# Deformable sampling on one core: tents in one VectorE operation, distances on GpSimd, and first weights, transposes and products placed earlier

## The reference

```python
xr = relu(x)                                     # x: normed input, B=8, C=32, H=W=16
om = conv3x3(xr, w_off) + b_off                  # 54 channels: 3 x (DG=2 groups) x (9 taps)
o1, o2, m = split(om, 3, axis=1)
ys = o1 + base_y;  xs = o2 + base_x              # where each tap of each position samples
mask = sigmoid(m)
sampled = bilinear(xr, ys, xs)                   # 0 outside the image
sampled = sampled * mask
out = einsum('bgcphw,ogcp->bohw', sampled, w) + b
out = (out - mean(out)) * rsqrt(var(out) + 1e-5) * gamma + beta
```

## Time and profile before

| | us |
|---|---|
| median of three runs | 128.83 |
| span of the profiled execution | 127.3 |
| first offsets written | 57.65 |
| first part of step 0's weights begins | 63.82 |
| transposes of step 3 begin | 74.31 |
| transposes of step 11 begin | 99.40 |
| batch statistics begin | 105.23 |

### The profile page before, as it was taken

How to read it: one execution, slowest core, us unless ns; L and a number is a source line. 1 busy time by engine, 2 the same in 40 slices (tenths; PEclk the granted TensorE clock), 3 DMA queues, 4 the chain that set the end, 5 groups by cost and what they waited for, 6 DMA issues and landing times.

```text
span 127.3 us, 3032 instructions
## 1 busy us (share of the span) xinstructions
PE 114.2 (90%) x1200; PEld 82.3 (65%) x1201; DVE 74.4 (58%) x149; ACT 68.3 (54%) x121; POOL 25.9 (20%) x34
## 2 busy tenths in 40 slices
PE   6989889998989899997977899999999987989990
PEld 5667566577423325877966678888888975656750
DVE  0076976718984362129999599699493004346241
ACT  4254796357630407027978959969956631347000
POOL 8996000004940000002616050050000000000000
PEclk9999999999999999999999999999999999999997
DMA  3544000000101000000000000000000000000002
GB/s 106 168 56 110 12 0 5 0 1 8 34 0 31 3 17 14 5 5 0 0 0 5 0 0 5 0 0 5 0 8 0 0 8 0 0 0 0 5 0 88
DMA packets 3060, 2.22 MB, mean 17 GB/s; under 512 B 1570, under 2 KB 2754, under 8 KB 3040
## 3 DMA queue, kind: packets, MB, share of 16 engines
q0 software_dynamic: 464, 0.67, 2.7%
q1 hardware_dynamic: 2144, 0.74, 2.4%
q10 hardware_dynamic: 432, 0.55, 1.2%
HBM read 1.68 MB, written 0.26 MB: 15 GB/s over the span
## 4 chain that ended last, share of the span: by engine, by line
PE 59%; DVE 21%; ACT 12%; issue 6%; DVEq 0%; ACTq 0%
PE ps L977 9%; PE ps L489 5%; DVE smat L913 5%; PE ps L991 5%; PE ps L1001 4%; PE ps L1293 4%; PE ps L514 3%; PE ps L496 3%; PE ps L276 3%; PE ps L287 3%; ACT tx L848 2%; DVE smatT L740 2%; PE ps L518 2%; PE ps L655 2%; ACT rstd L530 2%
## 5 line engine op out<-in xcount | busy, mean ns | idle before, releaser
L913 DVE TENSOR_TENSOR smat<-ty,tx 128x1536 f32<-128x1536 f32 (+1 forms) x14 | 21.5, 1555 | 4.3 <-ACT tx L848 4.2
L954 ACT ACTIVATE smatT<-ps 128x1536 f32<-128x1536 f32 x12 | 17.4, 1450 | 7.8 <-PE ps L977 7.6
L977 PE MATMUL ps<-cst,smat 128*128 128x128 f32 x144 | 18.1, 275 | 2.6 <-DVE smat L913 2.3
L977 PEld LDWEIGHTS ps<-cst,smat 128*128 128x128 f32 x144 | 15.7, 140 | 4.3 <-DVE smat L913 3.2
L489 PE MATMUL ps<-cst 128*128 128x256 f32 x48 | 13.0, 387 | 0.3 <-issue 0.3
L1001 PE MATMUL ps<-samp,wc 128*128 128x128 f32 x72 | 11.0, 291 | 0.0
L991 PE MATMUL ps<-smatT,xt 128*32 128x96 f32 x384 | 10.4, 249 | 0.4 <-ACT samp L945 0.4
L1001 PEld LDWEIGHTS ps<-samp,wc 128*128 128x128 f32 x72 | 8.9, 191 | 1.6
L489 PEld LDWEIGHTS ps<-cst 128*128 128x128 f32 x48 | 8.3, 190 | 2.2 <-issue 1.3
L830 POOL TENSOR_SCALAR disty<-disty 128x288 f32<-128x288 f32 x3 | 6.2, 2081 | 17.2 <-ACT disty L837 17.2
L991 PEld LDWEIGHTS ps<-smatT,xt 128*32 128x32 f32 x384 | 7.9, 109 | 2.3 <-issue 1.8
(11 more groups left out here) (200 smaller groups left out, 198.1 us busy)
## 6 DMA issues: line engine op xcount, KB each, us to landing
cst<-in_cst ACTq DMA_DIRECT2D x1, 278.0 KB, 3.5
x<-in_x SPq DMA_DIRECT2D x2, 128.0 KB, 2.9
ew<-in_L_ffn_weight POOLq DMA_DIRECT2D x4, 64.0 KB, 2.2
ew<-in_L_ffn_weight POOLq DMA_DIRECT2D x1, 256.0 KB, 4.2
w<-in_L_ffn_ffn_w SPq DMA_DIRECT2D x3, 64.0 KB
cst<-in_cst ACTq DMA_DIRECT2D x1, 129.0 KB, 3.0
out<-fin SPq DMA_DIRECT2D x1, 128.0 KB, 2.2
out<-fin ACTq DMA_DIRECT2D x1, 128.0 KB, 2.1
```

The costliest lines, as they stand in the source:

```text
L913: return nc.vector.tensor_tensor(smat[:, n % 3, BP * part.start:BP * part.stop, :].rearrange("p u (g r c) -> p (u g) r c", g=DG, c=W), ty[ ...
L954: nc.scalar.activation(smatT[:, n % 2, :, :, :].rearrange("p k g n -> p (k g n)"), ps[:, bank:bank + 3, :].rearrange("p b n -> p (b n)"), ...
L977: last = nc.tensor.transpose(ps[:, bank + u // BP, (u % BP) * P:(u % BP + 1) * P], smat[:, n % 3, u, :], ident)
```

## The change

- **Tents by one VectorE operation.** Distances are now to grid - 1, so d = offset - grid + 1, and `nearness` writes min(2 - d, d) in one `scalar_tensor_tensor`, which is 1 - |offset - grid| without the clipping at 0. Row weights clip (`max` with 0, then times mask). Columns stay unclipped; ScalarE's copy of the turned weights uses Relu instead of Copy, which clips the product. For `jh` = 0 the row tents are ScalarE's, clipped, in two passes.
- **Distances on GpSimd.** `distances_pool` makes all row distances and all column distances, but for those of `jh` = 0 that step 0 needs (`HEAD`, a third, 384 elements), which VectorE makes itself. It waits for `c_oms` of each `jh`. The rest of `jh` = 0 is `TAIL`, 768 elements.
- **Masks.** The sigmoid is Exp, Ln, Exp, three ScalarE operations, one set for `jh` = 0 and one for the other three together.
- **Order.** Six of the window transposes of `jh` = 0 go ahead of the 3x3 convolution, one filler matmul less before them. All window sets are copied by ScalarE. Window sets 1 to 3 go ahead of the fit's transpose. Step 0's transposes and ScalarE's copy of them go ahead of the branch, as do step 1's weights. Step 0's products come before the transposes of step 1. Two `keep_clock` calls of two matmuls go away. PSUM banks are dealt anew (`OMBANK`, `WINBANK`, `FITBANK`, `fit_bank`, `PARTS`).

The diff, cut to its core:

```diff
-OMBANK = (4, 0)
-WINBANK = (5, 1)
+OMBANK = (4, 3)
+WINBANK = (5, 0)
+FITBANK = 3
+PARTS = (1, 2, 0)
+EARLY = 6
...
+        HEAD, TAIL = slice(0, KBG // K), slice(KBG // K, KBG)
+        def column_distances(eng, jh, us, done):
+            shape = [P, us.stop - us.start, W]
+            eng.tensor_tensor(tx[:, jh, us, :], om[:, jh, 1, us].unsqueeze(2).broadcast_to(shape),
+                              const("grid").unsqueeze(1).broadcast_to(shape), ALU.subtract).then_inc(sem(done), 1)
...
+        def distances_pool(pool):
+            pool.wait_ge(sem("c_oms"), 1)
+            row_distances(nc.gpsimd, 0, "p_dy")
+            column_distances(nc.gpsimd, 0, TAIL, "p_dx")
             for jh in range(1, J * NH):
-                pool.wait_ge(sem("p_ay"), jh)
-                d = disty[:, jh, :, :]
-                nc.gpsimd.tensor_scalar(d, d, 1.0, 1.0, ALU.min, ALU.subtract).then_inc(sem("p_ty"), 1)
+                pool.wait_ge(sem("c_oms"), jh + 1)
+                row_distances(nc.gpsimd, jh, "p_dy")
+                column_distances(nc.gpsimd, jh, ALL, "p_dx")
+        def nearness(d, done):
+            nc.vector.scalar_tensor_tensor(out=d, in0=d, scalar=2.0, in1=d, op0=ALU.subtract, op1=ALU.min,
+                                           reverse0=True).then_inc(sem(done), 1)
...
+        def sigmoid_masks(act, link, part):
+            link(nc.scalar.activation(msk[:, part, :], om[:, part, 2, :], ACT.Exp, scale=-1.0))
+            link(nc.scalar.activation(msk[:, part, :], msk[:, part, :], ACT.Ln, bias=1.0))
+            nc.scalar.activation(msk[:, part, :], msk[:, part, :], ACT.Exp, scale=-1.0).then_inc(sem("c_me"), 1)
...
         def fit_dve(dve):
-            for n in range(1, NSTEP):
+            for n in range(2, NSTEP):
                 jh, ki = n // K, n % K
                 if ki == 0:
-                    dve.wait_ge(sem("p_tx"), jh)
+                    dve.wait_ge(sem("s_tx"), jh + 2)
                     dve.wait_ge(sem("s_ty"), jh + 1)
                 if n >= 3:
                     dve.wait_ge(sem("f_tr"), n - 2)
                 step_weights(n).then_inc(sem("f_w"), 1)
-                if ki == 0 and jh + 1 < J * NH:
-                    column_distances(nc.vector, jh + 1, "s_dx")
-                elif ki == 1 and jh + 1 < J * NH:
-                    sigmoid_mask(dve, link, jh + 1)
-                    if jh + 2 < J * NH:
-                        row_distances(nc.vector, jh + 2, "s_dy")
-                elif ki == 2 and jh + 1 < J * NH:
+                if ki == 2 and jh + 1 < J * NH:
+                    columns(dve, jh + 1)
+                    rows(dve, jh + 1)
                     row_weights(dve, jh + 1)
...
-            transposes(0)
-            for n in range(NSTEP):
+            products(0)
+            fit_transposes(pe, 1)
+            for n in range(1, NSTEP):
                 if n + 1 < NSTEP:
-                    transposes(n + 1)
+                    fit_transposes(pe, n + 1)
                 products(n)
-                if n:
-                    convolve(n - 1)
+                convolve(n - 1)
             convolve(NSTEP - 1)
...
             channels_first(0)
             channels_first(2)
-            exp_mask(0)
-            tent_y(act)
             windows(0)
-            abs_x(act)
-            relu_x(act)
-            windows(2)
-            windows(3)
+            act.wait_ge(sem("c_oms"), 1)
+            sigmoid_masks(act, masks_link, slice(0, 1))
+            first_rows(act, masks_link)
             for jh in range(1, J * NH):
-                exp_mask(jh)
+                windows(jh)
+            turned_weights(act, 0)
+            act.wait_ge(sem("c_oms"), J * NH)
+            sigmoid_masks(act, masks_link, slice(1, J * NH))
             by_fit(act, fit_act, wide_act)
...
-            keep_long(2, 5)
+            keep_long(1, 5)
             pe.wait_ge(sem("c_wd"), 1)
+            pe.wait_ge(sem("c_u"), 1)
+            window_transposes(0, WINBANK[0], range(EARLY))
             pe.wait_ge(sem("c_u"), J)
...
-            window_transposes(0, WINBANK[0], range(6))
+            window_transposes(0, WINBANK[0], range(EARLY, 12)).then_inc(sem("c_xt"), 1)
             positions_first(0)
-            window_transposes(0, WINBANK[0], range(6, 12)).then_inc(sem("c_xt"), 1)
             positions_first(1)
-            window_transposes(1, WINBANK[1]).then_inc(sem("c_xt"), 1)
+            window_transposes(1, WINBANK[1], range(9)).then_inc(sem("c_xt"), 1)
             pe.wait_ge(sem("f_xta"), DG)
-            window_transposes(2, WINBANK[0]).then_inc(sem("c_xt"), 1)
+            window_transposes(2, WINBANK[0], range(12)).then_inc(sem("c_xt"), 1)
+            pe.wait_ge(sem("f_xta"), 2 * DG)
+            window_transposes(3, WINBANK[1], range(9)).then_inc(sem("c_xt"), 1)
             pe.wait_ge(sem("c_fitp"), 1)
-            nc.tensor.transpose(ps[0:1, 0, 0:P], fitm[:, 0:1], ident).then_inc(sem("c_fitt"), 1)
-            keep_clock(2, 4)
-            pe.wait_ge(sem("f_xtd"), DG)
-            window_transposes(3, WINBANK[1]).then_inc(sem("c_xt"), 1)
-            keep_clock(2, 4)
+            nc.tensor.transpose(ps[0:1, FITBANK, 0:P], fitm[:, 0:1], ident).then_inc(sem("c_fitt"), 1)
+            fit_transposes(pe, 0)
...
             offsets(0)
             dve.wait_ge(sem("c_oms"), 1)
-            first_distances()
-            offsets(1)
-            offsets(2)
-            offsets(3)
-            dve.wait_ge(sem("c_oms"), 4)
+            head_columns(dve)
+            for jh in range(1, J * NH):
+                offsets(jh)
+            dve.wait_ge(sem("c_oms"), J * NH)
...
             row_weights(dve, 0)
             dve.wait_ge(sem("s_ty"), 1)
             dve.wait_ge(sem("s_tx"), 1)
-            first_weights(slice(0, 1))
+            for part in PARTS[:2]:
+                first_weights(slice(part, part + 1))
             dve.wait_ge(sem("c_fitt"), 1)
...
-            first_weights(slice(1, 2))
-            first_weights(slice(2, K3))
+            first_weights(slice(PARTS[2], PARTS[2] + 1))
+            tail_columns(dve)
+            dve.wait_ge(sem("s_tx"), 2)
+            second_weights()
             by_fit(dve, fit_dve, wide_dve)
```

More of the change, by code:

```diff
@@ L832, in abs_rows @@
[L832 to L855, removed]
+        YSHAPE = [P, KBG, SROWS]
+        gridy = const("gridy").unsqueeze(1).broadcast_to(YSHAPE)
@@ new lines, in head_columns, with tail_columns, columns, rows @@
+        def head_columns(dve):
+            column_distances(nc.vector, 0, HEAD, "s_dx")
+            dve.wait_ge(sem("s_dx"), 1)
+            nearness(tx[:, 0, HEAD, :], "s_tx")
+        def tail_columns(dve):
+            dve.wait_ge(sem("p_dx"), 1)
+            nearness(tx[:, 0, TAIL, :], "s_tx")
+        def columns(dve, jh):
+            dve.wait_ge(sem("p_dx"), jh + 1)
+            nearness(tx[:, jh, :, :], "s_tx")
+        def rows(dve, jh):
+            dve.wait_ge(sem("p_dy"), jh + 1)
+            nearness(disty[:, jh, :, :], "s_ny")
@@ L965, in fit_act @@
-            keep(NSTEP - 1)
-        def fit_pe(pe):
-            def transposes(n):
-                bank = 3 * (n % 2)
-                if n:
-                    pe.wait_ge(sem("f_w"), n)
-                if n >= 2:
-                    pe.wait_ge(sem("f_smt"), n - 1)
-                for u in range(K * BP):
-                    if n == 0 and u % BP == 0:
-                        pe.wait_ge(sem("f_w0"), u // BP + 1)
-                    last = nc.tensor.transpose(ps[:, bank + u // BP, (u % BP) * P:(u % BP + 1) * P],
-                                               smat[:, n % 3, u, :], ident)
-                last.then_inc(sem("f_tr"), 1)
+            keep(0)
@@ new lines, in fit_act, with fit_transposes @@
+            turned_weights(act, 1)
+            for n in range(2, NSTEP):
+                turned_weights(act, n)
+                keep(n - 1)
+            keep(NSTEP - 1)
+        def fit_transposes(pe, n):
+            bank = fit_bank(n)
+            if n:
+                pe.wait_ge(sem("f_w"), n)
+            else:
+                pe.wait_ge(sem("c_oms"), J * NH)
+            if n == 1:
+                pe.wait_ge(sem("f_xta"), DG * J * NH)
+            if n >= 2:
+                pe.wait_ge(sem("f_smt"), n - 1)
+            for i, part in enumerate(PARTS):
+                if n == 0:
+                    pe.wait_ge(sem("f_w0"), i + 1)
+                    if bank + part == WINBANK[0]:
+                        pe.wait_ge(sem("f_xta"), DG * (J * NH - 1))
+                for bp in range(BP):
+                    last = nc.tensor.transpose(ps[:, bank + part, bp * P:(bp + 1) * P],
+                                               smat[:, n % 3, part * BP + bp, :], ident)
+            last.then_inc(sem("f_tr"), 1)
@@ L1020, in wide_dve @@
             dve.wait_ge(sem("f_w0"), K3)
-            for jh in range(2, J * NH):
-                row_distances(nc.vector, jh, "s_dy")
-                column_distances(nc.vector, jh, "s_dx")
```

(8 more changed lines are left out.)

117 lines of the change are left out of this document (40 added, 77 removed).

## The result

| | before | after |
|---|---|---|
| median, four runs each, us | 128.94 (128.76 to 129.32) | 133.05 (132.47 to 133.41) |
| ratio to before | 1 | 1.030, 95% interval 1.0265 to 1.0337 |
| profiled execution's span, us | 127.3 | 131.0 |
| first offsets written | 57.65 | 57.22 |
| weights of step 3 ready | 74.27 | 77.95 |

The changed kernel is 3% slower, close to the 131.8 us forecast. Where transposes begin is read from the chain of waits, which counts them from the end of the work ahead; in the timeline the first of step 3 starts at 79.33, beside the last tap weights. The first thing to read is VectorE's chain: its timeline in the kernel after, from the first offsets to step 3's weights (columns as in the earlier trace rows).

What follows compares the result with a forecast made beforehand. Step 3's start, set by VectorE's chain, bounds the kernel, then TensorE's pace. Weights at 72.3 + 6.25 of GpSimd holds = 78.55, statistics 108.25, span 130.3, plus 1.5: 131.8 us; range 125.6 to 135.0.

Steps and rivals of the forecast that it cites:

- What bounds the kernel: Sampling loop: step 3's start sets the time, then TensorE's pace of 2.98 us a step; 29.67 us from there to statistics.
- The front: Six window transposes ahead of the 3x3 convolution: first offsets at 57.65 again, gain 0, up to 0.2 us lost.
- VectorE's chain at its own lengths: First offsets to step 3's weights with nothing in the way: ready at 72.3 against 74.26; 3.2 us gained, 125.6 us.
- GpSimd's reads: Two-input VectorE operations wait for GpSimd's distance reads: 0.45 rows, 1.2 tail, 1.8 columns; weights of step 3 at 78.55.
- less 0.4 and 0.1: Deductions from the summed holds: 0.4 us of the fit's wait that they cover, 0.1 us of hand-overs.
- the 0.23 of 1.04: Before: weights beside GpSimd's row clipping took 0.23 us longer, while it went on for 1.04; basis for pricing holds.
- Other edits: ScalarE's window sets, step 0's products and copy moved, masks by Exp, Ln, Exp, fewer fillers: nobody waits, no added cost.
- The clock put at 0: Fewer fillers with TensorE gaps between 62 and 78: cost 0, up to 2.98 us if it restarts at lower clock.
- The sum: Step 3's weights at 78.55, statistics at 108.25, span 130.3; plus 1.5 us outside the span, 131.8 us.
- Rival 1: GpSimd holds VectorE 0.23 us a meeting (126.7 us) or not at all (125.6, statistics 102.0); chance 0.28, at 126.2.
- Rival 2: GpSimd doesn't let go between queued operations: step 3's weights at 81.0, statistics at 110.7, 134.3 us; chance 0.18.
- Rival 3: VectorE mostly wins its turns, about half the holds remain: step 3 starts near 75.5, 128.8 us; chance 0.08.

Runs made afterwards that it cites:

- experiment 5: Changed kernel with the old order ahead of the offsets: two long fillers, no window transposes ahead of the convolution; 133.03 us in one execution.
- experiment 1: Changed kernel with GpSimd's distances replaced by constant writes of about the same duration that read nothing (output meaningless); 125.45 us, 0.969 of the kernel before.
- experiment 2: Changed kernel with eleven 256-column filler matmuls in TensorE's gaps before step 3; 131.88 us, 1.019 of the kernel before.
- experiment 7: Experiment 4's kernel with ScalarE's row tents ahead of its copy, and the tail's column distances on GpSimd from the second offsets on; 126.77 us, ratio 0.981.
- experiment 4: Changed kernel with all distances on VectorE, absolute values and row tents on ScalarE, a one-input subtraction on VectorE, some reordering; 127.98 us, 0.989 of before.

## Why the prediction was right, and where it was off

**What bounds the kernel** was right: everything is settled by when step 3 starts, and from there TensorE runs at its own pace. Step 3 to statistics took 109.12 - 79.49 = 29.63 us; the sum had 29.67.

**The front** was wrong by 0.43 us, in the good direction. The step "gain 0, the offsets come at 57.65 again" counted the six transposes and overlooked the convolution's own 4.46 us, which became 3.98; experiment 5 puts this on the new order ahead of it.

**VectorE's chain at its own lengths** was right. From the first offsets to step 3's weights the sum had 14.65 us (57.65 to 72.3); without holds experiment 1 has 14.27 (57.18 to 71.45). Pricing the tent by L862's line held: 0.56, 0.94 and 1.35 for 384, 768 and 1152 elements. The kernel before took 16.62 (57.65 to 74.27), so the edits would be worth 2.35 us there if GpSimd's distances held nobody.

**GpSimd's reads** were the right mechanism, turn by turn, at nearly the right price, with single meetings in other places:

| VectorE's operation | hold in the sum | hold measured |
|---|---|---|
| head tents | 0.4 | 0.38 (0.94 less 0.56) |
| row weights of `jh` = 0 | 0.35 | 0 (0.45) |
| first and second part of step 0's weights | 2.2 | 2.33 (3.62 less 1.29) |
| third part | 1.3 | 0.14 (0.81 less 0.67) |
| tail tents | 0.4 | 1.96 (2.90 less 0.94) |
| weights of steps 1 and 2 | 1.8 | 2.33 (5.76 less 3.43) |
| sum | 6.45 | 7.1 |

Three steps were off.

- The sum made each operation wait for the other's reads; the rows show it waiting for the end of the other's operation. That is 1.95 for a column pass, not 1.8, and makes 0.45 over three. The price came close only because reads at 0.23 for 288 elements, a figure taken from a GpSimd operation with one input (L830), fill 1.8 of the 2.16 us.
- The sum let GpSimd's passes start as if VectorE never held them: in the rows of after, a column pass lasts 2.59 and 3.66 instead of 2.16. The second one thus fell on the tail tents and not on the third part, a row pass on step 1's weights, and the last column pass on step 2's.
- The addition slipped: the terms make 6.45, and less 0.4 and 0.1 that is 5.95, where the sum went on with 6.25. By its terms step 3's weights come at 78.25, and the time is 131.5 us.

On the path the holds cost 77.95 - 57.22 - 14.27 = 6.46 us; that is less than the 7.1 of the table, mostly since 0.58 of wait for the fit's transpose, which experiment 1 has, falls away. So step 3's weights were ready at 77.95 against a forecast 78.55: 0.43 by the front, 0.38 by the own lengths and 0.30 by the slip, less 0.51 by the holds.

The Trainium skill ("SBUF — State Buffer", section "Who interferes with whom") says that a VectorE instruction with two SBUF inputs contends with GpSimd instructions that read SBUF and not with those that only write. Experiment 1 agrees (nothing held beside memsets). On the length of a hold the rows side with the whole instruction that the prediction quotes, and against the 0.23 of 1.04 that it read from L830: two-input passes hold to their end. As holds that is 1.95 of 2.16 for columns and 0.39 of 0.70 for rows, since two operations that take turns overlap a little in their records. Why L830, with one input, held so little no run shows.

**Other edits.** Masks, ScalarE's window sets and the moved products cost nothing on VectorE's path, as forecast: behind the first offsets its rows show no wait. The clock put at 0 was the worst step: the text saw the gaps between 62 and 78 and gave 2.98 as the bound, and 1.3 to 1.5 came true (1.32 in the statistics of experiment 2; 79.49 - 77.95 = 1.54 between weights and step 3, where 0.05 was forecast).

**The sum.** Statistics were forecast at 108.25 and came at 109.12: 0.60 earlier weights, 1.49 more wait for TensorE. The profiled execution took 132.93, which is 1.9 us beyond its span where the sum added 1.5. So the miss of 1.25 us against the median is mainly the clock, 1.49, and 0.4 outside the span, less the 0.60 of earlier weights. That it is so small is in part luck: the early front, the short chain and the slip against the longer holds and the clock.

**The rivals.** Rival 1 (no or small holds) is refuted by the first weights' rows; its lower price, with statistics at 102.0, is close to what experiment 1 gives when the reads are taken away (101.33). Rival 2 (GpSimd keeps VectorE out over several passes) is refuted: each of VectorE's operations is held by one pass, even with the next GpSimd pass queued right behind it. The 5.00 of the earlier trace rows is another kind of meeting, and nothing here shows why it lasts so long. Rival 3 (half of the holds) is refuted by their sum.

Where the time went from before to after, up to the statistics: -0.43 front, -2.35 shorter chain, +6.46 holds, +1.50 TensorE's later start behind the weights, and -1.29 in the loop, where no hand-over is left; together +3.89, as the table at the top has it.

## What to carry to other kernels

That GpSimd's queue is idle doesn't make work moved there free: look at what VectorE runs in that stretch. Beside additions with one operand in PSUM and beside a reduction over one SBUF operand, GpSimd's reads cost nothing (experiment 7). That isn't shown for every one-input operation: L854, a small `tensor_scalar`, took 0.47 us instead of 0.18 beside them in the kernel before. Beside two-input operations they cost nearly their whole length (1.95 of 2.16 us). Then the work is better given to ScalarE, or made one-input (0.75 instead of 1.36 us in experiment 4, with GpSimd idle). When an upstream delay opens gaps in TensorE's work, price the clock in the same sum, and when it is closed look at once for the next wait: experiments 4 and 7 each met a new one.

## What the runs showed of the hardware that was not expected

- A convolution of 144 small matmuls takes 3.98 to 4.02 us with transposes directly ahead of it, and 4.46 (before) and 4.68 (experiment 5) behind a pause of 0.22 and 0.23 us. Most of the loss isn't at its start: some 3.1 us into it the loading of its weights stops for 0.30 us (until 54.94) and 0.52 us (until 55.03), with no wait that the profile shows. Why was not tried.
- VectorE and GpSimd alternate strictly, operation by operation, when both read two SBUF operands: through the eight passes of the changed kernel, whichever comes second waits for the end of the other's operation. Both are stretched: a 2.16 us GpSimd pass becomes 2.59 or 3.66.
- TensorE's granted clock averaged 0.52 from 73.9 to 79.3 although it was busy 5.34 of 5.40 us there; it was back at 1.00 behind that. In experiment 1 TensorE also stood idle for 1.63 us ahead of step 0's products, with the clock at 1.00 throughout; which idle time costs the clock these runs don't settle.
